# Reordering the start of a recommender interaction kernel: D through ScalarE alone, three stores on GpSimd, and the gathers in two rounds

## The reference

```python
base = inputs                      # (512, 40, 16)
curr = base
for Wk, bk in zip([W0, W1, W2], [b0, b1, b2]):
    z = jnp.einsum('bid,bjd->bdij', base, curr)
    curr = jnp.einsum('bdij,ijh->bhd', z, Wk) + bk[None, :, None]     # h = 100
    logit.append(curr)
pooled = jnp.sum(jnp.concatenate(logit, axis=1), axis=-1)
out = pooled @ lin_w + lin_b       # (512, 1)
```

## Time and profile before

| | us |
|---|---|
| median of 3 runs | 183.70 (183.63 to 183.77) |
| the profiled execution | 184.18 |
| its span, first to last instruction | 182.3 |
| PE busy | 175.8 |
| DVE busy | 152.7 |
| ACT busy | 72.7 |
| POOL busy | 10.8 |

### The profile page before, as it was taken

How to read it: one execution, slowest core, us unless ns; L and a number is a source line. 1 busy time by engine, 2 the same in 40 slices (tenths; PEclk the granted TensorE clock), 3 DMA queues, 4 the chain that set the end, 5 groups by cost and what they waited for, 6 DMA issues and landing times.

```text
span 182.3 us, 2523 instructions
## 1 busy us (share of the span) xinstructions
PE 175.8 (96%) x798; PEld 119.1 (65%) x798; DVE 152.7 (84%) x140; ACT 72.7 (40%) x77; POOL 10.8 (6%) x17
## 2 busy tenths in 40 slices
PE   7998986999999999999999999999999999999994
PEld 2364454777777777767777777777777777677760
DVE  0699962379999999999999999999999999995022
ACT  2555250044464246424642464246424642440021
POOL 3630120400000000000000000000000000000000
DMA  5997556699978577957795879477847760000000
GB/s 189 395 412 281 131 167 151 226 417 409 374 245 293 162 227 231 281 173 237 225 305 158 231 223 313 153 224 235 304 150 230 229 205 0 0 4 0 0 0 0
DMA packets 12198, 37.32 MB, mean 205 GB/s; under 512 B 2497, under 2 KB 3421, under 8 KB 12190
## 3 DMA queue, kind: packets, MB, share of 16 engines
q1 hardware_dynamic: 11026, 36.36, 60.8%
q10 hardware_dynamic: 1164, 0.86, 2.0%
HBM read 35.88 MB, written 1.33 MB: 204 GB/s over the span
## 4 chain that ended last, share of the span: by engine, by line
PE 87%; DMA 3%; DVE 3%; SPq 2%; issue 2%; ACTq 1%; ACT 0%; POOL 0%; DVEq 0%; POOLq 0%
PE q_ps L456 41%; PE c_ps L456 37%; PE q_ps L509 4%; SPq L165 2%; DMA d_dram<-w_d 2%; DMA pair_sb<-d_dram 2%; DVE xb_z L248 1%; PE q_ps L548 1%; PE c_ps L500 1%; PE q_ps L465 1%; PE c_ps L598 1%; ACTq L159 1%; PE c_ps L601 0%; PE q_ps L551 0%; DVE acc L325 0%
## 5 line engine op out<-in xcount | busy, mean ns | idle before, releaser
L336 ACT ACTIVATE z_high<-xb_z 126x1024 fp32r<-126x1024 f32 x56 | 59.3, 1061 | 81.9 <-DVE xb_z L248 81.8
L255 DVE TENSOR_TENSOR z_low<-xb_z,z_high 126x1024 fp32r<-126x1024 f32 x56 | 68.3, 1222 | 1.1 <-ACT z_high L336 1.0
L248 DVE TENSOR_TENSOR xb_z<-x_a,xb_z 126x1024 f32<-126x1024 f32 x50 | 60.9, 1217 | 9.3 <-DMA xb_z<-xw 9.3
L456 PE MATMUL c_ps<-z_high,wc_high 126*101 126x512 f32 x112 | 35.3, 396 | 0.6 <-POOL wc_low L427 0.6
L456 PE MATMUL q_ps<-z_high,wq_high 126*101 126x512 f32 x108 | 34.0, 396 | 1.4 <-DVE wq_low L290 1.4
L456 PE MATMUL c_ps<-z_low,wc_high 126*101 126x512 f32 x112 | 35.1, 395 | 0.0
L456 PE MATMUL c_ps<-z_high,wc_low 126*101 126x512 f32 x112 | 35.0, 394 | 0.0
L456 PE MATMUL q_ps<-z_high,wq_low 126*101 126x512 f32 x108 | 33.8, 394 | 0.0
L456 PE MATMUL q_ps<-z_low,wq_high 126*101 126x512 f32 x108 | 33.7, 393 | 0.0
L456 PEld LDWEIGHTS c_ps<-z_high,wc_high 126*101 126x101 f32 x112 | 18.4, 166 | 8.3 <-POOL wc_low L427 1.2
L456 PEld LDWEIGHTS q_ps<-z_high,wq_high 126*101 126x101 f32 x108 | 17.8, 166 | 8.8 <-DVE wq_low L290 1.8
(11 more groups left out here) (56 smaller groups left out, 61.5 us busy)
## 6 DMA issues: line engine op xcount, KB each, us to landing
xb_z<-xw SPq DMA_DIRECT2D x50, 512.0 KB, 4.4
x_a<-xa SPq DMA_DIRECT2D x8, 512.0 KB, 5.0
w_post<-w1x SPq DMA_DIRECT2D x4, 512.0 KB, 8.3
w_d<-w2h SPq DMA_DIRECT2D x4, 404.0 KB, 5.9
pair_sb<-w_pairs SPq DMA_DIRECT2D x1, 404.0 KB, 10.0
d_dram<-w_d SPq DMA_DIRECT2D x3, 126.2 KB, 4.0
d_dram<-w_d SPq DMA_DIRECT2D x1, 252.5 KB, 3.3
d_dram<-w_d ACTq DMA_DIRECT2D x1, 252.5 KB, 4.0
```

The costliest lines, as they stand in the source:

```text
L248: nc.vector.tensor_tensor(xb_z[0:K, c, :], x_a[0:K, u % 2, :], x_b, ALU.mult).then_inc(z_done, 1)
L255: nc.vector.tensor_tensor(z_low[0:K, m % SLOTS, :], xb_z[0:K, c, :], z_high[0:K, m % SLOTS, :].bitcast(fp32), ALU.subtract).then_inc(low_d ...
L336: nc.scalar.activation(z_high[0:K, m % SLOTS, :], xb_z[0:K, m % C, :], ACT.Copy).then_inc(high_done, 1)
L456: last = nc.tensor.matmul(ps[0:J, h * B:(h + 1) * B], w[0:K, c * J:(c + 1) * J], z[0:K, slot, h * B:(h + 1) * B], start=(c == 0 and k == 0 ...
```

## The change

The first unit's order is written anew on four engines.

- PE: the selections of chunks 3 to 6 are moved behind the making of V and between the groups of D.
- DVE copies no group of D any more. It forms chunks 1 to 6 in another order and splits chunks 3 to 6 behind them.
- ACT copies all five groups, rounds only chunk 2 between them and chunk 3 behind them, and issues no store. It then rounds 4, 5 and 6 and issues its gathers.
- Seven stores go by SP, with 48 rows where they had 64, and three by POOL: the duplicates of the wrapped columns. POOL issues two of them ahead of the third `sum_w0` and one behind it.
- The gathers of piece 1 are issued only when those of piece 0 have landed. SP issues four of piece 0 and ACT two; each issues three of piece 1.

```diff
+DB = 48
+DS_SP, DS_POOL = 7, 3
-GATHER = [(side, t, piece) for piece in range(len(WQ_CUTS) - 1) for t in range(T) for side in range(2)]
+GATHER = [(side, t, piece) for piece in range(len(WQ_CUTS) - 1) for side in range(2) for t in range(T)]
+GATHER_SP = [g for g in GATHER if g[0] == 0] + [(1, 0, 0)]
...
@@ sync @@
             sp.wait_ge(dgroup_copied, 1)
-            store_d(sp, 0, LEFT + 4 * GI, 4 * GI, LOWER - 4 * GI, (0, DR))
-            sp.wait_ge(dgroup_copied, 2)
-            sp.wait_ge(dgroup_copied_dve, 1)
-            store_d(sp, 0, LEFT, 0, 2 * GI, (0, DR))
-            store_d(sp, 0, LEFT + F, 0, RIGHT, (32, DR))
+            store_d(sp, 0, LEFT + 4 * GI, 4 * GI, LOWER - 4 * GI, (8, 8 + DB))
             sp.wait_ge(dgroup_copied, 3)
...
+            store_d(sp, 0, LEFT, 0, 2 * GI, (0, DB))
+            store_d(sp, 1, LEFT + UPPER_AT[0], 0, 2 * GI, (DR - DB, DR))
+            sp.wait_ge(dgroup_copied, 4)
+            store_d(sp, 0, LEFT + 2 * GI, 2 * GI, GI, (0, DB))
+            store_d(sp, 1, LEFT + UPPER_AT[2], 2 * GI, GI, (DR - DB, DR))
+            sp.wait_ge(dgroup_copied, 5)
+            store_d(sp, 0, LEFT + 3 * GI, 3 * GI, GI, (4, 4 + DB))
+            store_d(sp, 1, LEFT + UPPER_AT[3], 3 * GI, GI, (10, 10 + DB))
             sp.wait_ge(equals_cleared, 1)
-            sp.wait_ge(d_stored, 16 * DS)
+            sp.wait_ge(d_stored, 16 * DS_SP)
+            sp.wait_ge(d_stored_pool, 16 * DS_POOL)
             for side, t, piece in GATHER:
-                if side == 0:
+                if (side, t, piece) == (0, 0, 1):
+                    sp.wait_ge(dpair_loaded[0], 16 * 2 * T)
+                if (side, t, piece) in GATHER_SP:
                     gather_d(sp, side, t, piece)
@@ gpsimd @@
             low_w0(1)
+            pool.wait_ge(dgroup_copied, 3)
+            store_d(pool, 0, LEFT + F, 0, RIGHT, (32, DR), d_stored_pool)
+            store_d(pool, 1, LEFT - 2 * GI, 0, 2 * GI, (0, 32), d_stored_pool)
             sum_w0(2)
+            pool.wait_ge(dgroup_copied, 4)
+            store_d(pool, 1, 0, 3 * GI - (LEFT - 2 * GI), LEFT - 2 * GI, (0, 32), d_stored_pool)
             low_w0(2)
```

More of the change, by code:

```diff
@@ L42 @@
 DW = LEFT + F + RIGHT
-DS = 10
+DB = 48
+DS_SP, DS_POOL = 7, 3
 WC_CUTS = (0, 1, 3, C)
@@ L127, in build @@
         small_loaded, selected = sem("small_loaded"), sem("selected")
-        d_stored = sem("d_stored")
+        d_stored, d_stored_pool = sem("d_stored"), sem("d_stored_pool")
         dpair_loaded = [sem(f"dpair_loaded{i}") for i in range(len(WQ_CUTS) - 1)]
@@ L135, in build @@
         dgroup_done, dgroup_copied = sem("dgroup_done"), sem("dgroup_copied")
-        dgroup_copied_dve = sem("dgroup_copied_dve")
         wc_sums, wc_highs, wc_ready = sem("wc_sums"), sem("wc_highs"), sem("wc_ready")
@@ L160, in gather_d, with store_d @@
                          ).then_inc(dpair_loaded[piece], 16)
-        def store_d(eng, upper, column, first, n, rows):
+        def store_d(eng, upper, column, first, n, rows, stored=d_stored):
             r0, r1 = rows
             eng.dma_start(d_dram[r0:r1, column * J:(column + n) * J],
-                         w2_d[DR * upper + r0:DR * upper + r1, first * J:(first + n) * J]).then_inc(d_stored, 16)
+                         w2_d[DR * upper + r0:DR * upper + r1, first * J:(first + n) * J]).then_inc(stored, 16)
         def chunks(tile, c0, c1):
@@ L275, in split_x @@
                                         ALU.subtract).then_inc(xa_split, 1)
-            def copy_d(g):
-                dve.wait_ge(dgroup_done, D_ORDER.index(g) + 1)
-                nc.vector.tensor_copy(w2_d[:, g * GI * J:(g + 1) * GI * J], d_ps[0]).then_inc(dgroup_copied_dve, 1)
             def first_weights(i):
@@ L291, in first_weights, with products @@
                                         ALU.subtract).then_inc(wq_ready, 1)
[L293 to L301, removed]
-                    form(it, m)
[L303 to L307, removed]
+            def products(it, m0, m1):
+                for m in range(m0, m1):
+                    form(it, m)
                     if m >= PRODUCT_AT and (m - PRODUCT_AT) % C == 0:
                         product(it, (m - PRODUCT_AT) // C)
-                    if m > 1 and m != C:
+                    if m > C:
                         split(it, m - 1)
-            products(0, 0)
+            form(0, 0)
+            split_x()
+            split(0, 0)
+            form(0, 1)
+            form(0, 2)
+            split(0, 1)
+            form(0, 3)
+            form(0, 4)
+            form(0, 5)
+            split(0, 2)
+            form(0, 6)
+            for m in range(3, C):
+                split(0, m)
+            first_weights(0)
+            first_weights(1)
+            products(0, C, 2 * C)
             with dve.Fori(0, NCH // BODY - 1) as it:
-                products(it, BODY)
+                products(it, BODY, 2 * BODY)
             split(0, NCH - 1)
@@ L365, in _ @@
             round_high(0, 1)
-            round_high(0, 2)
             act.wait_ge(v_multiplied, 1)
@@ L373, in _ @@
                                  scale=float(D)).then_inc(const_copied, 1)
-            round_high(0, 3)
             copy_d(4)
             copy_d(0)
-            round_high(0, 4)
+            copy_d(1)
+            round_high(0, 2)
             copy_d(2)
[L379 to L384, removed]
+            copy_d(3)
+            round_high(0, 3)
             cast_w0(2)
-            act.wait_ge(dgroup_copied, 3)
-            act.wait_ge(dgroup_copied_dve, 2)
-            for m in range(5, BODY):
+            for m in range(4, BODY):
                 if m == GATHER_AT:
                     act.wait_ge(equals_cleared, 1)
-                    act.wait_ge(d_stored, 16 * DS)
+                    act.wait_ge(d_stored, 16 * DS_SP)
+                    act.wait_ge(d_stored_pool, 16 * DS_POOL)
                     for side, t, piece in GATHER:
-                        if side == 1:
+                        if (side, t, piece) == (1, 0, 1):
+                            act.wait_ge(dpair_loaded[0], 16 * 2 * T)
+                        if (side, t, piece) not in GATHER_SP:
                             gather_d(act, side, t, piece)
@@ L539, in d_group @@
                 pe.wait_ge(w1_loaded[g], 16)
[L540 to L545, removed]
+                if place > 1:
+                    pe.wait_ge(dgroup_copied, place - 1)
                 n = (GI if g < NG - 1 else 1) * J
@@ L560, in _ @@
             v_piece(0)
+            v_piece(1)
             c1_chunk(0, 0)
-            select_xb(3)
-            v_piece(1)
-            select_xb(4)
             v_piece(2)
@@ L567, in _ @@
             constant()
-            select_xb(5)
+            select_xb(3)
             turn_v()
+            select_xb(4)
             d_group(4)
@@ L572, in _ @@
             d_group(1)
+            select_xb(5)
             d_group(2)
+            select_xb(6)
             d_group(3)
-            select_xb(6)
             for m in range(1, C):
```

5 lines of the change are left out of this document (removed).

## The result

The changed kernel takes 182.98 us (median of 5 executions, 182.67 to 183.19) against 183.74 of the kernel before (183.63 to 183.85, 5 executions): a ratio of 0.9956, 95% interval 0.9941 to 0.9970, 0.76 us faster. The prediction said 182.4 within 181.3 to 184.4, faster with a chance of 0.69. The profiled execution took 183.19, its span is 181.4, and the clock was granted in full.

What follows compares the result with a forecast made beforehand. PE was taken as the bound, so time follows c1_chunk(7)'s start: 41.45 to 40.2 by the later of two paths, 1.25 less. Median 183.70 - 1.25 = 182.45, stated as 182.4, range 181.3 to 184.4.

Steps and rivals of the forecast that it cites:

- the two paths: Weights through first_weights to q_chunk(2), giving 40.2, and loads of unit 1 through split(7), giving 40.0; both end at c1_chunk(7).
- the kind of the new wait: PE would idle at q_chunk(2), with wq_low as releaser, by 1 to 2 us, instead of at q_chunk(0).
- The start of the gathers: ACT reaches its gathers at 24.95, behind its last round; before, gathers started at 26.36; stores landed by 23.4.
- T1 - T0: From the gathers' start to piece 0's landing: forecast 24.95 to 27.3, a small transfer landing 1.8 after issue.
- T2 - T1: From piece 0's landing to piece 1's: 4.0 us, as 0.6 to first data, 2.9 of packets, 0.4 for last landing.
- the second round's price: Gathers' start to piece 1's landing would take 6.3 us instead of 6.0, costing 0.3.
- the second round is dearer: Rival, 13%: piece 1 takes over 5.2 us after piece 0's landing (break-even); at 6.0 the time is 184.5.
- path B: Loads of unit 1, issued once all gathers landed, through split(7): c1_chunk(7) at piece 1's landing plus 8.7, 40.0.
- PE's own path: PE's work up to q_chunk(0): c1_chunk(3) waits for low_w0 until 22.95, the seventh chunk ends at 28.55.
- its cover: Slack for POOL's store issues: at 1.5 us each the cast slips 0.2; each further 0.5 an issue delays gathers 1.0.
- ACT's 2.82 us of store issues: ACT's time spent issuing three stores before; removing it was to bring the gathers' start 1.4 us forward.
- The selections' new place: On PE, two selections between groups of D were said to eat more than half of the 1.4 us from earlier V.

Runs made afterwards that it cites:

- the one-round kernel: The changed kernel without the wait between the two rounds of gathers, so SP issues seven and ACT five at once: 181.52 us, ratio 0.9887 to the kernel before.
- The late round of SP's three: From the changed kernel with the wait between gather rounds kept on SP alone, ACT issuing its five at once: 182.30 us, ratio 0.9932 to the kernel before.
- the duplicates on SP: The changed kernel with POOL's three stores of the duplicates issued by SP instead, two rounds of gathers kept: 182.87 us, ratio 0.9953 to the kernel before.
- selections early: The one-round kernel with PE's order of selections, pieces of V and groups of D as before the change: 182.68 us, ratio 0.9955 to the kernel before.

## Why the prediction was right, and where its sum was not

The direction, the two paths and the kind of the new wait were right. c1_chunk(7) was forecast at 40.2 and came at 40.51. But this small error is the sum of three larger ones that cancel, and that they cancel is luck.

1. *The start of the gathers, -1.2.* I had ACT reach them at 24.95, when its engine has ended round 6. They were issued at 23.78, while the rounds ran until 21.76 + 2.94 = 24.70: ACT's sequencer, which hands the instructions out, issues a DMA while the engine still works on what was handed to it. What released them was POOL's clearing, at 23.76. The stores had landed by then: the last was issued at 20.9 and took 2.3, which is 23.2. My 23.4 for that was right.
2. *T1 - T0, +0.6.* I had SP's four gathers issued ahead of ACT's two. Both began at 23.78, SP's fourth at 25.0, and T1 was 1.7 behind that, close to a small store's 1.8.
3. *T2 - T1, +0.9.* This is the mis-sized term: 4.0 in the prediction, 31.61 - 26.7 = 4.9 measured. The packets took 3.2 us where I had 2.9, and the ends 0.7 and 1.0 where I had 0.6 and 0.4; the wait for the last landing is the larger part of the error. With T1 - T0 the two rounds took 7.8 and not 6.3, so the second round's price was not 0.3 but about 1.8. The run of the kernel before with the waits alone shows it directly: 185.53, where my term would give 183.9. The rival "the second round is dearer" was right about the mechanism; it stayed under its break-even of 5.2 only by 0.3, and the early T0 paid for it. Had piece 0 landed at my 27.3, the measured 4.9 would have put T2 at 32.2 and c1_chunk(7) at 32.2 + 1.83 + 7.07 = 41.1, a gain of 0.35 and not of the forecast's 1.25. The rest of the measured 0.94 came from the first error.
4. *From T2 on, nothing.* q_chunk(2) at T2 + 1.83, five q_chunks in 7.07, path B 0.2 ahead: as worked out.
5. *PE's own path, +0.65, at no cost.* I had q_chunk(0) at 28.55, it came at 29.20: low_w0 took 1.56 us where I had 0.97, so c1_chunk(3) started at 23.57 and not 22.95. PE's wait at q_chunk(2) was therefore 1.29 and not 1.8. It hid in that wait here, and it is what bounds the one-round kernel.

The Trainium skill (DMA: Bandwidth & Descriptors, Anatomy of one DMA), cited with that rival, puts a fixed part of about 2 us into every transfer that GpSimd issues, most of it behind the data. The gathers here are issued by SP and ACT. The late round of SP's three agrees with the 2 us, 3.0 us for 0.94 of work, but not with where they lie: 0.8 stood ahead of the first packet and 0.6 behind the last.

POOL's issue was taken as 1.0 and took 1.15 / 2 = 0.57, well inside its cover. ACT's 2.82 us of store issues as a source of the gain holds up in direction: putting three issues back costs 1.1 of the 2.1 us at full clock. The selections' new place, which I said was mostly eaten up, carries 1.1 to 1.2 in the one-round kernel, by the estimate above about half of it by itself. I had looked only at the last copy; the stores of the earlier groups and the split that follows round 2 and 3 were what it brought forward. These two don't simply add up, since both end at c1_chunk(3) or at T0.

The time itself was 182.98 for 182.4. Of the 0.6 left, 0.3 is c1_chunk(7), and the rest that the profiled execution lay 0.48 above the median before and 0.21 after.

## What to carry to other kernels

A wait for a first batch of transfers before the second is issued pays the time ahead of the first packet and behind the last once more (1.8 us in the kernel before), and can help only if the first batch is what is late; ask which landing the consumer's second step needs. When an early stage is moved forward, look for every later landing that is waited for, not only the first. When a kernel's executions fall into two groups, look at the granted clock behind TensorE's longest wait: here waits of 1.56 us and more cost more than their length in some executions.

## What the runs showed of the hardware

- *TensorE's clock.* After a wait of 3.06 us the granted clock fell to 0.50 (1.2 GHz) in the profiled execution, 0.2 us after TensorE was at work again, and all six executions had a mean clock of 0.991 or less. With a profiled wait of 1.83 us it fell in the same way. With profiled waits of 1.97, 1.83 and 1.56 us, 2 of 6, 6 of 12 and 4 of 12 executions had 0.991 or less and were 1.2 to 1.7 us slower than the rest of the same kernel. With 1.49 us (the duplicates on SP) none of six shows this, and with 1.29 us (the changed kernel) none of five. For executions that weren't profiled only the mean clock is known, not where it fell.
- *GpSimd beside VectorE.* low_w0 took 0.97 us before, and 1.56 or 1.68 where a split of VectorE ran beside it. Beside a form, which takes one input from PSUM, it took 0.97 again (selections early, from 21.88). The other way round, a split of 1.22 us took 2.49 beside sum_w0. By the Trainium skill (SBUF — State Buffer, SBUF: two separate sides), a VectorE instruction with two SBUF inputs and a GpSimd one that reads SBUF shut each other out for the whole instruction; the traces agree in kind; they don't show which of the two is held.
- *Loads beside gathers.* The loads of unit 1, 512 KB each, issued right behind the second round moved its landing by 1.6 us.
